# A transformer block on one core: the next image's latents, two rope groups and the first group's maxima as side work of the experts

## The reference, cut to what matters

```python
h = layernorm(x) * (1 + ca) + sa
kv_c = h @ W_kv;  kv_c = kv_c * rsqrt(mean(kv_c**2) + eps) * g_kv;  q_c = h @ W_q
q = concat(heads(q_c @ W_qdec, 16), rope(heads(q_c @ W_qrope, 32)))      # 16 heads
k = concat(heads(kv_c @ W_kdec, 16), rope(heads(h @ W_krope, 32)));  v = heads(kv_c @ W_vdec, 16)
x = x + ga * (softmax(causal(q @ k.T / sqrt(48))) @ v) @ W_o
t = (layernorm(x) * (1 + cb) + sb) @ Wm + bm, seen as 8 slices of 32 per token
w, i = top_2(softmax(t @ expert_emb))                                     # of 16 experts
comb = sum over the two of w * (gelu(t @ W1[i] + b1[i]) @ W2[i] + b2[i])
x = x + gb * (comb @ Wo + bo)
```

## Time and profile before

| | us |
|---|---|
| median of 3 runs | 3806.48 |
| profiled execution, its own time | 3810.99 |
| its span, first to last instruction | 3809.4 |
| TensorE busy | 3187.5 (84%) |
| weight loads busy (they overlap the matmuls) | 1420.2 (37%) |
| VectorE busy | 1980.1 (52%) |
| ScalarE busy | 1759.9 (46%) |
| GpSimd busy | 975.5 (26%) |

### The profile page before, as it was taken

One profiled execution on the slowest core, in us unless ns is written; L12 is line 12 of the kernel. 1 busy time (PEld: TensorE's weight loads), 2 busy tenths in 40 slices (PEclk: granted clock), 3 DMA queues, 4 the chain that ended last, 5 costly groups with the idle time before them and its releaser, 6 DMA issues. The chain is left out here.

```text
span 3809.4 us, 51685 instructions
## 1 busy us (share of the span) xinstructions
PE 3187.5 (84%) x17420; PEld 1420.2 (37%) x17420; DVE 1980.1 (52%) x4709; ACT 1759.9 (46%) x2098; POOL 975.5 (26%) x917
## 2 busy tenths in 40 slices
PE   3796987969889698796978979789797997979978
PEld 1333343433333334333333433334333343333433
DVE  3764447544465544645456454574445744456453
ACT  0153831548225482254813548135570446704466
POOL 1111421124311243112431124212242122321233
PEclk8998999989999898998989989899898998989989
DMA  3302422034220342104421043300434005240053
GB/s 98 66 2 65 134 66 57 2 88 123 65 46 2 98 119 64 40 1 105 122 63 31 1 116 111 76 19 2 127 100 93 2 1 138 89 93 1 5 141 94
DMA packets 141123, 253.97 MB, mean 67 GB/s; under 512 B 48789, under 2 KB 81445, under 8 KB 140717
## 3 DMA queue, kind: packets, MB, share of 16 engines
q1 hardware_dynamic: 139792, 248.07, 25.4%
q10 hardware_dynamic: 1024, 2.10, 0.3%
...
## 5 line engine op out<-in xcount | busy, mean ns | idle before, releaser
L814 ACT ACTIVATE pt<-ps 128x1024 f32<-128x1024 f32 (+3 forms) x768 | 607.2, 812 | 1054.6 <-PE ps L578 1043.6
L1189 ACT ACTIVATE hm<-ps 128x1024 f32<-128x1024 f32 x1024 | 966.7, 1030 | 135.3 <-PE ps L1145 114.3
L578 PE MATMUL ps<-q,k 49*128 49x512 f32 (+3 forms) x3072 | 643.2, 510 | 7.5 <-DMA q<-mr 6.4
L1131 PE MATMUL ps<-x,w1s 98*128 98x512 f32 x2048 | 627.8, 431 | 16.3 <-PEq L946 15.9
L1267 POOL TENSOR_TENSOR acc<-acc,gy 128x1024 f32<-128x1024 f32 x192 | 458.4, 2387 | 594.5 <-DVE gy L1230 593.3
L722 DVE CUSTOM_DVE_ANT_0 rt<-ps,maskd 128x128 f32<-128x128 f32 (+3 forms) x1024 | 462.1, 489 | 226.5 <-PE ps L605 202.5
L1145 PE MATMUL ps<-hm,w2s 128*32 128x512 f32 x4096 | 543.8, 604 | 1.3 <-ACT hm L1189 1.3
L605 PE MATMUL ps<-k,q 48*128 48x512 f32 (+3 forms) x1536 | 397.3, 505 | 170.5 <-DVE mx L722 121.1
L1131 PEld LDWEIGHTS ps<-x,w1s 98*128 98x128 f32 x2048 | 356.8, 194 | 483.3 <-ACT hm L1189 411.2
L868 POOL TENSOR_SCALAR_AFFINE_SELECT pt<-pt 128x256 f32<-128x256 f32 x512 | 206.1, 408 | 1257.8 <-ACT pt L814 1253.7
L1230 DVE SCALAR_TENSOR_TENSOR gy<-ps,b2c,gb 128x512 f32<-128x512 f32 x384 | 287.6, 751 | 461.1 <-PE ps L1145 460.3
...
## 6 DMA issues: line engine op xcount, KB each, us to landing
gb<-gate_rows SPq DMA_DIRECT2D x1024, 128.0 KB, 2.7
q<-rc SPq DMA_DIRECT2D x128, 128.0 KB, 2.4
k<-rc SPq DMA_DIRECT2D x128, 128.0 KB, 2.4
x<-thi SPq DMA_DIRECT2D x256, 64.0 KB, 2.0
...
k<-pt SPq DMA_DIRECT2D x128, 64.0 KB, 2.3
...
x<-tlo SPq DMA_DIRECT2D x128, 64.0 KB, 2.0
```

Source lines behind the costliest of these rows:

```text
L578: mm = pe.matmul(bank(2 * (u % 2) + hh)[:, 0:HALF - f], L.k2[rows, 2 * g + pr, j * P:(j + 1) * P].bitcast(F32), L.q2[rows, 2 * g + pr, c * ...
L814: nc.scalar.activation(L.pt[:, u % PTS, :, f:HALF], L.ps[:, 2 * (u % 2):2 * (u % 2) + 2, 0:HALF - f], ACT.Exp, scale=SCALE).then_inc(S["c_ ...
L1131: mm = pe.matmul(bank(2 * (u % 3) + c), L.w1s[:, e, :], L.x2[:, h, c * HALF:(c + 1) * HALF], start=True, stop=True)
L1189: nc.scalar.activation(L.hm[:, u % HM, :], bank(2 * (u % 3), 2), ACT.Gelu).then_inc(S["e_gelu"], 1)
```

## The change

The front of the next image leaves the attention stage. It is now a list of items (`front_items`): transposes, latents, ropes of groups 0 and 1, contents, then the 24 pairs of group 0's maxima and their row. `front_matmuls`, `front_vector`, `front_add`, `front_power` and `front_moves` do one item on one engine. Before the loop `stage_first` runs the list for the first image; in the loop the experts stage runs it for the next image (for the last image, the first one's again). The copies and squares that ScalarE did in the front are now VectorE's.

The experts run by token halves: first all experts for tokens 0 to 511, then for the others. A unit is one expert and two slices of one half, a step q is two units (four slices) with one second product; there are 64 steps. First products have two pairs of banks (three before), second products two banks, and the last two banks are the ring of the side items and of the output projections. `sum4` and its matmuls are gone: gated results are added one expert at a time into `ct` (60 adds of 512 columns on GpSimd, 24 of 1024 before). The items stand at steps 10 to 62; projections of the first four token tiles stand at steps 38 to 44, the other four at the end. `load_next` is issued before the first gate rows.

In the attention there are now 52 slots: the main work starts at slot 0, the maxima of group g+1 are packed into the first 9 of 12 slots, the four ropes of group g+2 into the next 2, and the filling is gone. The ropes' DMAs follow on SyncE, and TensorE waits for them in slots 12 and 24.

All tiles of the stages are cut from four fixed regions of SBUF (`Regions`). In the diff, `front_matmuls` and `front_vector` are shown for four kinds of items; the others are alike.

```diff
+def front_items():
+    items = [("ht", c, j) for c in range(2) for j in range(CH)]
+    items += [("qct", 0), ("qct", 1), ("kvt", 0), ("kvt", 1), ("rope", 0), ("rope", 1), ("sum",), ("rope", 2), ("rope", 3)]
+    items += [("qc", 0, 0), ("qc", 0, 1), ("std", 0), ("std", 1), ("kc", 0, 0), ("kc", 0, 1)]
+    items += [("v", k) for k in range(4)] + [("qc", 1, 0), ("qc", 1, 1), ("kc", 1, 0), ("kc", 1, 1)]
+    items += [("rope", r) for r in range(4, 8)] + [("pair", *p) for p in PAIRS] + [("row",)]
+    return items
...
+def ring_write(pe, L, R, item, k=0):
+    u = R.first(item) + k
+    if u >= 2:
+        pe.wait_ge(L.S["f_v"], u - 1)
+    return L.bank(6 + u % 2)
+def ring_read(v, L, R, item, k=0):
+    u = R.first(item) + k
+    v.wait_ge(L.S["f_p"], u + 1)
+    return L.bank(6 + u % 2)
...
+def front_matmuls(pe, L, R, item):
+    S, kind = L.S, item[0]
...
+    elif kind in ("qct", "kvt"):
+        c = item[1]
+        out = ring_write(pe, L, R, item)
+        pe.wait_ge(S["f_v"], R.after["ht", c, CH - 1])
+        w, rows = (L.wqs, P) if kind == "qct" else (L.wkvs, KVR)
+        for k in range(CH):
+            mm = pe.matmul(out[0:rows, :], w[:, k, :], L.ht[:, k, half(c)], start=(k == 0), stop=(k == CH - 1))
+        mm.then_inc(S["f_p"], 1)
+    elif kind == "rope":
+        out = ring_write(pe, L, R, item)
+        pe.wait_ge(S["f_v"], R.after["qct", item[1] % 2])
+        rope_matmuls(pe, L, item[1], out).then_inc(S["f_p"], 1)
...
+    elif kind == "pair":
+        i, n, pr = item[1:]
+        keys = key_range(i, n)
+        pe.wait_ge(S["f_mv0"], 16 * 2 * HG)
+        pe.wait_ge(S["f_cq"], 16 * HG)
+        pe.wait_ge(S["f_ck"], 16 * HG)
+        outs = [ring_write(pe, L, R, item, hh) for hh in range(2)]
+        for hh in range(2):
+            rows = slice(HP * hh, HP * hh + QD)
+            pe.matmul(outs[hh][:, 0:keys.stop - keys.start], L.q2[0][rows, pr, i * P:(i + 1) * P].bitcast(F32R),
+                      L.k2[0][rows, pr, keys].bitcast(F32R), start=True, stop=True).then_inc(S["f_p"], 1)
+    elif kind == "row":
+        out = ring_write(pe, L, R, item)
+        pe.wait_ge(S["f_mf"], 1)
+        pe.transpose(out[0:HG * NT, 0:P], L.mxf[:, 0, :], L.ident[:, :]).then_inc(S["f_p"], 1)
...
+def front_vector(v, L, R, item):
+    S, kind = L.S, item[0]
...
+    elif kind == "rope":
+        r = item[1]
+        tk = half(rope_of(r)[2])
+        src = ring_read(v, L, R, item)
+        if r >= 3:
+            v.wait_ge(S["f_add"], r - 2)
+        v.stream_shuffle(L.rt[:, r % 3, 1, :], src, SWAP).then_inc(S["f_sh"], 1)
+        v.tensor_tensor(L.rt[:, r % 3, 0, :], src, L.cos[:, tk], ALU.mult).then_inc(S["f_v"], 1)
+        v.wait_ge(S["f_sh"], r + 1)
+        v.tensor_tensor(L.rt[:, r % 3, 1, :], L.rt[:, r % 3, 1, :], L.sin[:, tk], ALU.mult).then_inc(S["f_rt"], 1)
...
+    elif kind == "pair":
+        i, n, pr = item[1:]
+        w = key_range(i, n).stop - n * HALF
+        for hh in range(2):
+            src = ring_read(v, L, R, item, hh)
+            dst = L.mx[:, 0, (2 * hh + pr) * NT + i, n:n + 1]
+            if n == i // 4:
...
+                                       scalar=-3e38, op0=ALU.add, op1=ALU.max, accum_out=dst).then_inc(S["f_v"], 1)
+            else:
+                v.tensor_reduce(dst, src[:, 0:w], AX.X, ALU.max).then_inc(S["f_v"], 1)
...
+def front_moves(sp, L, R, part):
+    S = L.S
+    if part == 0:
+        move_neg(sp, L, 0, S["f_ng"])
+        for k in range(2):
...
+        move_neg(sp, L, 1, S["f_ng"])
+        move_content(sp, L, 0, range(HG, 2 * HG), S["f_cc"])
+        move_content(sp, L, 1, range(HG, 2 * HG), S["f_cc"])
+        for k in range(2):
+            sp.wait_ge(S["f_add"], 4 + 2 * k + 2)
+            move_rope(sp, L, 1, k, S["f_mv1"])
...
 def stage_first(nc, L):
...
+        @block.tensor
+        def _(pe):
+            for item in items:
+                front_matmuls(pe, L, R, item)
...
     def side_parts(s):
-        g, n = s // NS, s % NS
+        g, n = s // NS + 1, s % NS
         parts = [[], []]
-        if g < NG:
-            for k in range(PER):
-                parts[k * 2 // PER].append(("pair", g, pairs[PER * n + k]))
-            if s == 0:
-                parts[0] = [("rope", r) for r in range(4, 4 * NG)] + parts[0]
+        if g < NG and n < PSLOTS:
+            mine = PAIRS[len(PAIRS) * n // PSLOTS:len(PAIRS) * (n + 1) // PSLOTS]
+            for k, p in enumerate(mine):
+                parts[k * 2 // len(mine)].append(("pair", g, p))
+        if g + 1 < NG and PSLOTS <= n < PSLOTS + 2:
+            for k in range(2):
+                parts[k].append(("rope", 4 * (g + 1) + 2 * (n - PSLOTS) + k))
         return parts
...
+                if s in (NS, 2 * NS):
+                    pe.wait_ge(S[f"p_mv{s // NS + 1}"], 16 * 2 * HG)
+                    pe.wait_ge(S["p_cq1"], 16 * 8)
+                    pe.wait_ge(S["p_ck1"], 16 * 8)
                 side(parts[0])
                 if now:
                     scores(*now, 1)
...
                 if before:
                     values(*before)
-                if s < NS + LAG:
-                    for _ in range(FILL):
-                        pe.matmul(bank(PVB), L.identb[:, :], L.identb[:, :].unsqueeze(1).broadcast_to([P, 4, P]),
-                                  start=True, stop=True)
...
                 now = main_step(s)
+                if now and diag[now[1]]:
+                    select(*now)
                 for part in side_parts(s):
                     for item in part:
                         if item[0] == "rope":
                             add(item[1])
-                if now and diag[now[1]]:
-                    select(*now)
...
-            sp.wait_ge(S["p_ng"], 32)
-            for g in range(NG):
-                move_row(g)
-            for g in range(NG):
+            for g in range(1, NG):
+                sp.wait_ge(S["c_rd"], ring_uses_to_row(g))
+                move_row(sp, L, g, S[f"c_row{g}"])
+                if g + 1 < NG:
+                    for k in range(2):
+                        sp.wait_ge(S["p_add"], 4 * (g - 1) + 2 * k + 2)
+                        move_rope(sp, L, g + 1, k, S[f"p_mv{g + 1}"])
...
-    EG = NE // 4
-    NQ = FH * EG
-    HM, GB, AC = 8, 4, 5
-    EARLY = 18
+    NU = 2 * 2 * NE * 2
+    NQ = NU // 2
+    HM, GB, GY = 4, 4, 3
+    L2 = 4
+    STATS, POWER, ROWS = 5, 6, 8
+    def unit(u):
+        return u // (4 * NE), u // (2 * NE) % 2, u // 2 % NE, u % 2
+    def schedule():
+        items = front_items()
+        slots = [[] for _ in range(NQ)]
+        first = [i for i in items if i[0] not in ("pair", "row") and not (i[0] == "rope" and i[1] >= 4)]
+        for k, item in enumerate(first):
+            slots[10 + max(k - 4, 0) + min(k, 4) // 2].append(item)
+        for k in range(4):
+            slots[37 + 2 * k].append(("rope", 4 + k))
+            slots[38 + 2 * k].append(("out", k))
+        for k, p in enumerate(PAIRS):
+            slots[37 + k].append(("pair", *p))
+        slots[62].append(("row",))
+        return slots
+    slots = schedule()
+    R = Ring([item for slot in slots for item in slot] + [("out", t) for t in range(4, NT)])
+    where = {item: q for q, slot in enumerate(slots) for item in slot}
...
         def _(pe):
             def inner(u):
-                h, e = u // NE, u % NE
-                if u >= 3:
-                    pe.wait_ge(S["e_gelu"], u - 2)
-                for c in range(2):
-                    mm = pe.matmul(bank(2 * (u % 3) + c), L.w1s[:, e, :], L.x2[:, h, c * HALF:(c + 1) * HALF],
+                c, j, e, p = unit(u)
+                if u >= 2:
+                    pe.wait_ge(S["e_gelu"], u - 1)
+                for k in range(2):
+                    mm = pe.matmul(bank(2 * (u % 2) + k), L.w1s[:, e, :], L.x2[:, c, 4 * j + 2 * p + k, :],
                                    start=True, stop=True)
                 mm.then_inc(S["e_l1"], 1)
...
-                eg = q % EG
-                pe.wait_ge(S["e_gelu"], 4 * (q + 1))
+            def outer(q):
+                e = unit(2 * q)[2]
+                pe.wait_ge(S["e_gelu"], 2 * q + 2)
+                if q >= 2:
+                    pe.wait_ge(S["e_gy"], q - 1)
+                for h in range(4):
+                    mm = pe.matmul(bank(L2 + q % 2)[FD * h:FD * h + FD, :], L.w2s[:, e, :],
+                                   L.hm[:, (2 * q + h // 2) % HM, (h % 2) * HALF:(h % 2 + 1) * HALF],
+                                   start=True, stop=True)
+                mm.then_inc(S["e_l2"], 1)
+            def project(t):
+                out = ring_write(pe, L, R, ("out", t))
+                pe.wait_ge(S["e_add"], 30 * (t // 4 + 1))
+                for k in range(CH):
+                    mm = pe.matmul(out[:, 0:C], L.ct[:, k, t * P:(t + 1) * P], L.wfg[:, k, :],
+                                   start=(k == 0), stop=(k == CH - 1))
+                mm.then_inc(S["f_p"], 1)
+            for q in range(NQ):
+                inner(2 * q)
```

(86 more changed lines are left out.)

722 lines of the change are left out of this document (365 added, 357 removed).

## The result

The changed kernel takes 3983.68 us, the median of 4 runs (3965.49 to 4002.69), beside 3808.77 (3805.4 to 3813.13) for the kernel before on the same chip: a ratio of 1.0459, with a 95% interval of 1.0407 to 1.0511. The prediction was 3643, faster with a chance of 0.88, and 3555 to 3775; the kernel is slower, and the time lies 209 us above the range. It lies 65 us above 3919 too, the sum of all terms at their upper ends. The profiled execution has a span of 3977.8 us against 3809.4, and TensorE's mean granted clock is 0.873 against 0.931.

What follows compares the result with a forecast made beforehand. TensorE was taken to bound the attention and experts. Per image 168.5 + 58.7 + 195.4 + 7.4 + 8.2 = 438.2 us instead of 468.6; 243 saved in eight images, less 80 for the first front: 3643, range 3555 to 3775.

Steps and rivals of the forecast that it cites:

- +3.0; bounds 0 and 6: Attention: TensorE's clock is low at the first scores and behind two DMA waits, costing 3.0 us an image.
- the +1.8 and +1.2: Attention: low clock costs 1.8 us at the first scores and 1.2 behind the two DMA waits, per image.
- The waits in slots 12 and 24: Attention: TensorE waits there for the ropes' DMAs, 5.0 us each, +10.0 an image; bounds 0 and 7.9 each.
- Crowding: Attention: 48 maxima in 9 slots, paced by VectorE, cost +4 us an image; bounds 0 and 12.
- Experts: Experts stage per image: TensorE-bound, takes on the next image's front; 195.4 us, then 7.4 end and 8.2 turn.
- The rule on weight loads: Experts: loads overlap only across differing row groups; switches would cost 10.7 us an image instead of 3, sum near 3705.
- The start: Experts: first gate rows come late because SyncE issues the next image's loads ahead; +2 us, bounds 0 and 5.
- Turn, end and routing: Per image: loop turn stays at 8.2 us, experts' end falls from 18.2 to 7.4, routing stays at 58.7.
- First front: Before the loop: the first image's front, hidden by nothing, costs 78 us once, say 80 (60 to 100).
- 48 maxima at about 0.58 (28): Before the loop, first image's front: 48 maxima at about 0.58 us each take 28 us.
- The slower rival: Experts, steps 10 to 62: TensorE waits for VectorE's side reads, 0.83 us a step, 42 per image, 3980; chance 0.09.

Runs made afterwards that it cites:

- e7: e3 with eight idle float32 products of 512 columns ahead of the attention's first product; 3784.10 us, ratio 0.9932.
- e3: The changed kernel with the ropes of group g+2 one each in slots 4 to 7, moved before the row; 3780.69 us, ratio 0.9925.
- e1: The changed kernel with five idle float32 products before TensorE's wait for the ropes' DMAs in slots 12 and 24; 3884.59 us, ratio 1.0197.
- e8: e5 with the pair ahead of the rope in steps 37 to 44 of the experts; 3855.32 us, ratio 1.0128.
- e6: e8 with the gate rows sent before the next image is loaded; 3839.39 us, ratio 1.0088.
- e5: e3 with the ropes in slots 0 to 3 and the 24 pairs cut unevenly over nine slots; 3882.34 us, ratio 1.0193.
- e4: The kernel before the change without its filling (FILL = 0), nothing else; 3792.44 us, ratio 0.9956.

## Why the prediction was wrong

**The attention's term "+3.0; bounds 0 and 6" is the step that failed.** The prediction saw that the first scores come after 8.2 us without matmuls and that the clock is then 0.50, priced 3.4 us of it and assumed that the clock is back after that, as it is at the start of the experts, whose stream is dense. (By rows 9 one such start costs 3.40 - 2.24 = 1.2 us, so three cost 3.5; the +1.8 and +1.2 are near that, but don't follow from it.) In the attention of after the clock is up for good only 34 us behind the first product, and 34 and 17 us behind the two waits, each time with a rise and a second fall in between. The warm price is known from e7 and e3: 50.4 + 47.7 + 41.5 + 26.9 = 166.5 us with ropes and side work, at 1.00 and without a DMA wait. After has 261.3 - 59.1 = 202.2. Of the 35.7 between them 8.9 are the waits themselves, 26.8 the clock and what the other order of the ropes may add. By experiment the clock behind the waits is 12.4 of it (e1) and the cold start 8.7 (e7, one image), 21.1 together; for the 5.7 left no run separates the clock from the order. Against the bound of 6, the clock is 15 to 21 us an image outside my range, and the range had no case for it. e3 takes both away by moving eight ropes and is 203 us faster.

- *The waits in slots 12 and 24:* right. +10.0 predicted, 71.2 / 8 = 8.9 measured, released by the DMA as written. What I missed is what stands behind them.
- *Crowding:* mis-sized. +4 taken, bounds 0 and 12; e7's and e3's 166.5 less 141.0 and 10.5 are 15.0, which is 11 an image more than taken, 3 outside the bound, and the second largest part of the miss. It is a remainder; no run changes the crowding alone. So the theory that the clock is the whole miss does not hold either. A group with side work took 37.6 before; group 2, which has no ropes, takes 41.5, and group 1 without its ropes' 5.3 takes 42.4. With the pairs in nine slots VectorE has 34 of 48 us, but the wait is in bursts (53.1 + 71.9 = 125 us of stands for VectorE in the attentions, 15.6 an image).
- *Experts:* 195.4 + 7.4 + 8.2 predicted, 216.4 measured. What was left out adds up to more than the 5.4, so other terms must have been a little too high; the runs don't tell which. The rule on weight loads, with 8 us more, is not borne out where pairs stand: such a step takes 2.55 us (1097.16 to 1099.71) and the next one without side work 2.12 (1102.26 to 1104.38), so a pair of 512 columns adds 0.43 (one of 128 columns 0.26), where 0.40 was taken for the products alone and the rule would add 0.21 for the switches. The 0.28 us of a record of 512 columns is no evidence for the rule either: the scores, with 49 rows and two row groups in turn, take the same (1.13 for four). A weight load of 128 columns takes 0.19 us in the trace (median of L1318's), not the 0.107 of the estimate. Missing was the ring of two banks where rope and pair share a step: (47.6 + 19.5) / 8 = 8.4 us of stands (49.5 less the 1.9 of the first front), forecast as none; but e8 shows that shrinking them does not shorten the stage in proportion. The start is the second. The first gating begins 11.2 us after the stage's first product, against 7.0 before: 4.2 late instead of 2, and e6 gives back 3.2. A third is a fall of the clock that no stand precedes: TensorE goes without a gap through the sixteen one-column records of the sum of squares (L528, 64x1, 1.94 us), and behind them, in six of the eight experts stages, the clock is at 0.50 for some 3.4 us (in the third image's rows 968.1 to 971.5), which makes four records of first products take 1.88 us instead of 1.20 and four rope records 2.87 instead of 1.88. VectorE's row in the timeline of after:

```profile
919.42 1.41 DVE L1408 SCALAR_TENSOR_TENSOR rest<-ps,b2c,wide 128x512 f32<-128x512 f32 x2 [10.67 <-DMA wide<-gate_rows]
```

- *Turn, end and routing:* right (end and turn 14.9, from 1110.0 to 1124.85, against 15.6; routing 59.1 against 58.7).
- *First front:* 78 predicted, 90.8 measured. The mis-sized term is "48 maxima at about 0.58 (28)": the maxima start at 101.0, where the forecast has them at 101.8, and end at 145.4, 44.4 us later. A pair fills both banks of the ring, so TensorE and VectorE take turns and neither works beside the other (VectorE's row, then TensorE's):

```profile
137.41 1.29 DVE L638 TENSOR_REDUCE front<-ps 128x1 f32<-128x512 f32 x2 [0.94 <-PE ps L565]
```

```profile
138.85 0.80 PE L565 MATMUL ps<-heads 48*128 48x512 f32 x2 [1.44 <-DVE front L638]
```

  The clock is 0.50 from 104 to 150 too, and two such records take 0.80 instead of 0.50 us (L565 at 1063.27), so at most 7 of the 16 us are the clock's.
- *The slower rival* named 3980, and the time is 3984. It is right by accident: its place was the experts and its price 42 us an image there; the experts lost 5.4. Its mechanism, TensorE kept waiting by VectorE's reads, appears in steps 37 to 44, in eight stands an image of 0.61 and 1.49 us in place of fifty of 0.83, and in the attention's first slots, where I had not put it.

The clock can be cross-checked for the whole run. By the mean granted clock the lower level holds for 2 x (1 - 0.873) x 3977.8 = 1010 us in after, 2 x (1 - 0.931) x 3809.4 = 526 before, and 2 x (1 - 0.910) x 3768.5 = 678 in e3. From after to e3 that is 332 us less. The Trainium skill (TensorE: Matmul & The Clock Gate, Part 1, HAM oscillation — how this bites in real kernels) prices low time at half of it, which by its rule is an estimate of 166 us here; with the 71 us of waits that makes 237, where the profiled spans differ by 209. The Trainium skill, in the same page's next section (A second HAM failure mode: psum-queue depth-cycling), says that frequent short stands between groups of products can make the clock swing; e5's fall behind stands of 0.84 to 0.88 us agrees with it, and e3's equal stands without a fall show that it is no rule to count by. e4 shows the limit of such a price: its clock is 0.890, 834 us or so at the lower level, and it is faster than before. In such a stretch TensorE is busy for only half of the time (22.17 of 44.30 us) and mostly stands for VectorE.

Reading the profile before, I could have had a sign of it. The earlier trace rows shows 0.91, 0.71 and 0.72 in the three stretches where TensorE is partly idle, and 1.00 and 0.99 where it is dense. The new attention was forecast with gaps of 5 us and bursts of side products, hence as a stretch of the first kind, and was priced as one of the second.
